# Moving the per-chunk sums over d from place 9 to place 13 in a three-layer cross network kernel

## The chip, the cores and the metric

The kernel runs on one core of a Trainium2 chip. The metric is the device time of one execution in microseconds. Three timed executions of the kernel before gave 656.12, 654.75 and 654.58 us, with a median of 654.75 us. A fourth execution was profiled. Its instructions span 655.7 us and its own time was 657.29 us.

## What is computed

A batch of 512 rows looks up 39 embedding tables and gets x0, of shape (512, 39, 16): batch b, field f, dimension d. Three cross layers follow, each with 128 maps, and the result of each is summed over d. Then comes a small dense network. Cut to what matters:

```python
x0 = xk = e                                   # (512, 39, 16)
for W in (f0, f1, f2):
    z = einsum('bfd,bgd->bfgd', x0, xk).reshape(b, f * g, d)
    cur = einsum('bpd,pm->bmd', z, W)         # (512, 128, 16)
    outs.append(cur); xk = cur
z = sum(concatenate(outs, axis=1), axis=-1)   # over d
h = relu([z, dense_ctx] @ W_top1 + b_top1)
h = relu(h @ W_top2 + b_top2)
y = h @ W_top3
```

Everything is float32. The output is (512, 1).

## The kernel before

**Tiling.** The batch is cut into 16 chunks c of 32 rows (CHUNKS, CB). A chunk has 32 x 16 = 512 columns (b, d). It is cut again into four subs s of 8 rows, which are 128 (b, d) pairs each. Four chunks make a quarter of 128 rows.

**Layer 1** is the main work. For a sub, x1 (128 maps by 128 pairs) is multiplied with w1 for all 39 fields. The 39 x 128 result columns are produced in 10 strips of four fields (the last has three). So a chunk has SLOTS = 40 places n, one strip at each. A strip is three matmuls, high and low parts of the operands (L988, L989, L992). It is written to one of Y_BANKS = 7 PSUM banks, used in turn. Each strip is then multiplied with x0 per field and added into x2. ScalarE (ACT) does strips 0, 3, 5 and 8 of a sub (BY_ACT, L859). VectorE (DVE) does the other six (L718). Its first one, strip 1, starts from the tile that ACT writes from strip 0 (`first`). GpSimd (POOL) adds up the parts (L584 twice, L591, L594) and writes the finished x2 of the sub, transposed, into the tile x2_t (L600; the profile prints x_t for it and for x0_t). POOL also issues the table gathers (L574), until three chunks before the end.

**Layer 0** of the next chunk is woven into the same 40 places. DVE makes six products z at places 9, 12, 15, 18, 21 and 24 (L649), one more at place 6 (L660) and a correction at 27 (L671). TensorE uses them at places 15 to 33 (L948, L935). TensorE also turns x0 at place 6 (L957). Around places 35 to 38, ACT and DVE take the result apart (L803, L691, L696).

**The sums.** Layer 2 is linear in x2, and only its sum over d is wanted. So the kernel first forms g_sum[g, f, b], the sum over d of x2 times x0, and multiplies with w2 afterwards. For chunk c-1 this is `sum_products(c - 1)` (L1006): 32 small matmuls, into four PSUM banks of the same ring of seven (TILES = 4). It stands in front of strip SUMS_AT = 9 of chunk c in TensorE's order. It waits for x2_t of the last sub of chunk c-1 (x2_t_ready), for x0_diag, and, by `drained`, for the four banks that it overwrites. ACT copies the four banks to g_sum in `keep_g` (L826), which stands at the same place in ACT's order. POOL may write x2_t of the first sub of chunk c only when the sums have read the old one (g_ready).

**Layer 2** (L1019, 39 matmuls) is done for a whole quarter at place 13 of chunks 4, 8 and 12 (`closes_quarter`), and for the last quarter after the loop. It needs g_sum of its last chunk.

**Order.** All of this is written out by hand, engine by engine. Every engine executes its list in order and waits on semaphores. There is no planner. The ring positions come from `slot_of_strip` and `slot_of_sums`: strip q sits in slot q + 4 x (sums before it), and its bank is the slot modulo 7. With the sums at place p, the four banks they need were last used by strips p-7 to p-4, and the three strips after the sums reuse those of strips p-3 to p-1.

Of the kernel before, what the change touches and what calls it, by code (L numbers as in the profile page):

```python
# [19 lines left out]
CHUNKS = BATCH // CB  # L20
# [12 lines left out]
PER_QUARTER = CHUNKS // QUARTERS  # L33
# [43 lines left out]
def part_of(c, s):  # L77

    return c + HALVES - 1 if c else s * HALVES // SUBS
# [104 lines left out]
TILE_ROWS = P // TILES  # L184
TILE_B = SB // TILES
TILE_COLUMNS = TILE_B * FG
SUMS_AT = 9
LAST_SUMS_AT = 38
SUMS_OF = [(c, 0, SUBS) for c in range(CHUNKS - 1)] + [(CHUNKS - 1, 0, SUBS - 1), (CHUNKS - 1, SUBS - 1, SUBS)]


def sums_before(q):

    c, n = q // SLOTS, q % SLOTS
    return (c - 1 if c else 0) + (c > 0 and n >= SUMS_AT) + (c == CHUNKS - 1 and n >= LAST_SUMS_AT)


def slot_of_strip(q):

    return q + TILES * sums_before(q)  # L200


def slot_of_sums(e):
    if e == CHUNKS:
        return SLOTS * CHUNKS + TILES * e
    c, at = (e + 1, SUMS_AT) if e < CHUNKS - 1 else (CHUNKS - 1, LAST_SUMS_AT)
    return SLOTS * c + at + TILES * e


STRIP_IN = {slot_of_strip(q): q for q in range(SLOTS * CHUNKS)}  # L210
SUMS_IN = {slot_of_sums(e) + t: (e, t) for e in range(CHUNKS + 1) for t in range(TILES)}


def closes_quarter(c):

    return c > 0 and c % PER_QUARTER == 0


def layer0_at(c):


    plans = []
    if c == 0:
        plans.append((1, PRODUCT0_HALF_AT, LAYER0_HALF_AT, *TURN_X0_HALF_AT, *X1_HALF_AT))
    if c + 1 < CHUNKS:
        product_at, layer_at = PRODUCT0_AT, LAYER0_AT
        if c == 0:
            product_at, layer_at = PRODUCT0_FIRST_AT, LAYER0_FIRST_AT
        elif closes_quarter(c):
            product_at, layer_at = PRODUCT0_LATE_AT, LAYER0_LATE_AT  # L230
        plans.append((part_of(c + 1, 0), product_at, layer_at,
                      *(TURN_X0_AT if c else TURN_X0_LATE_AT), *X1_AT))
    return plans
# [6 lines left out]
def build_program(nc, a):  # L240
    with ExitStack() as ctx:
# [531 lines left out]
        def _(act):  # L773
            def high_last(i):
                k = i - STACKED_FROM
                act.wait_ge(z0_last_ready, k + 1)

                at_least(act, z0_stack_ready, k)
                act.copy(z0_last_hi[:], z0_last[:]).then_inc(z0_last_hi_ready, 1)

            def parts_of_w0_last():
                act.wait_ge(w0_last_ready, 1)
                act.copy(w0_last_hi[:], w0_last[:]).then_inc(w0_last_hi_ready, 1)
                act.wait_ge(w0_last_hi_ready, 1)
                act.wait_ge(roles_in, 16)
                act.activation(w0_last_signed[:], w0_last_hi[:].bitcast(F32), ACT.Copy, scale=roles[:, 1:2]
                               ).then_inc(w0_signed_ready, 1)

            def diagonal(c):
                act.wait_ge(x0_t_ready, part_of(c, SUBS - 1) + 1)  # L790
                act.wait_ge(mask_in, 16)

                at_least(act, g_ready, c)
                for b in range(TILE_B):
                    last = act.activation(x0_diag[:, :, b, 0:FIELDS], x0_t[:, c % 2, :, :], ACT.Copy,
                                          scale=mask[:, b:b + 1])
                last.then_inc(diag_ready, 1)

            def high_x1(i):

                at_least(act, strip_ready, SLOTS * (chunk_of(i) - 1))
                act.wait_ge(l0_step, T0 * i + T0)
                act.copy(x1_hi[:, chunk_of(i) % 2, columns_of(i)], acc0[:, columns_of(i)]).then_inc(x1_hi_ready, 1)  # L803

            def keep_x0_t(i):
                c, subs = chunk_of(i), subs_of(i)

                at_least(act, scale_step, scaled_before(SUBS * (c - 1), 0) if c else 0)
                at_least(act, diag_ready, c - 1)
                act.wait_ge(x0_t_turned, i + 1)  # L810
                act.copy(x0_t[:, c % 2, subs[0]:subs[-1] + 1, :],
                         x0_t_bank[i > 0][:, subs[0]:subs[-1] + 1, 0:FIELDS]).then_inc(x0_t_ready, 1)

            def keep_g(e):

                c, begin, end = SUMS_OF[e]
                act.wait_ge(g_ready, e + 1)
                if begin == 0 and closes_quarter(c):

                    act.wait_ge(out1_ready, c // PER_QUARTER)  # L820
                    act.wait_ge(out2_done, c // PER_QUARTER)
                at = c % PER_QUARTER * CB
                kept = g_sum[:, :, at + SB * begin:at + SB * end].rearrange("g f (s t b) -> g t f s b", t=TILES, b=TILE_B)
                for t in range(TILES):
                    found_sums = strip_flat[:, (slot_of_sums(e) + t) % Y_BANKS, 0:TILE_COLUMNS * (end - begin)]
                    act.copy(kept[:, t, :, :, :], found_sums.rearrange("g (s b f) -> g f s b", b=TILE_B, f=FG)  # L826
                             ).then_inc(g_kept, 1)

            def keep_out1(quarter):
                act.wait_ge(g_kept, kept_of_quarter(quarter))  # L830
                act.copy(out1[:, P * quarter:P * quarter + P], g_sum[:, FIELDS, :]).then_inc(out1_ready, 1)

            def keep_out2(quarter):
                act.wait_ge(out2_done, quarter + 1)
                act.copy(out2[:, P * quarter:P * quarter + P], acc2[quarter]).then_inc(out2_ready, 1)
# [53 lines left out]
            for c in range(CHUNKS):  # L889
                for n in range(SLOTS):  # L890
                    s, g = n // STRIPS, n % STRIPS
                    for i, _, _, _, keep_at, high_at, _, _ in layer0_at(c):
                        if n == high_at:
                            high_x1(i)
                        if n == keep_at:
                            keep_x0_t(i)
                    if (STACKED_FROM <= part_of(c + 1, 0) < X0_PARTS
                            and n == (STACK_LATE_AT if closes_quarter(c) else STACK_AT)[1]):
                        high_last(part_of(c + 1, 0))
                    if (c, n) == W0_STACK_AT:  # L900
                        parts_of_w0_last()
                    if n == DIAGONAL_AT:
                        diagonal(c)
                    if c and n == SUMS_AT:
                        keep_g(c - 1)
                    if c == CHUNKS - 1 and n == LAST_SUMS_AT:
                        keep_g(c)
                    if closes_quarter(c) and n == KEEP_OUT1_AT:
                        keep_out1(c // PER_QUARTER - 1)
                    if closes_quarter(c) and n == KEEP_OUT2_AT:  # L910
                        keep_out2(c // PER_QUARTER - 1)
                    if g in BY_ACT[s]:
                        scale(c, s, g)
# [14 lines left out]
        def _(pe):  # L928
# [22 lines left out]
            def turn_x0(i):  # L951
                c = chunk_of(i)
                pe.wait_ge(once_in[c % 2], 16 * arrivals(i))

                at_least(pe, out0_ready, i)
                for s in subs_of(i):
                    last = pe.transpose(x0_t_bank[i > 0][:, s, :], x0_once[:, c % 2, P * s:P * s + P], ident[:])  # L957
                last.then_inc(x0_t_turned, 1)
# [35 lines left out]
            def sum_products(e):  # L994

                c, begin, end = SUMS_OF[e]
                slot = slot_of_sums(e)
# [45 lines left out]
            for c in range(CHUNKS):  # L1043
                for n in range(SLOTS):
                    s, g = n // STRIPS, n % STRIPS
                    for i, _, layer_at, turn_at, _, _, _, _ in layer0_at(c):
                        if n in layer_at:
                            layer0(i, layer_at.index(n))
                        if n == turn_at:
                            turn_x0(i)  # L1050
                    if c and n == SUMS_AT:
                        sum_products(c - 1)
                    if c == CHUNKS - 1 and n == LAST_SUMS_AT:
                        sum_products(c)
                    if closes_quarter(c) and n == LAYER2_AT:
                        layer2(c // PER_QUARTER - 1)
                    layer1(c, s, g)
# [115 lines left out]
```

## Time and profile before

| what | value |
|---|---|
| median of three executions | 654.75 us (654.58 to 656.12) |
| profiled execution: its own time, its span | 657.29 us, 655.7 us |
| PE busy | 619.1 us, 94% of the span |
| DVE busy | 536.5 us, 82% |
| POOL busy | 515.2 us, 79% |
| ACT busy | 357.9 us, 55% |
| chain that ended last | PE 72%, POOL 18% of the span |
| DMA | 48.86 MB, mean 75 GB/s |

PE is TensorE's matmuls and PEld its weight loads. The profile gives TensorE's granted clock as 0.984 of full speed over the span. In the 40 slices PE shows 9 tenths from the fourth to the last but one. DVE and POOL also show 8 and 9 in most slices. They fall to 5 and 7 tenths in three groups of slices: there TensorE does layer 2 and nothing arrives for them. The chain is the work that ended last, followed back from the end.

### The profile page before, as it was taken

Reading aid. Unit: us, or ns where it says so; the run is one execution under the profiler, and the core shown is the slowest. Engines: PE = TensorE matmul, PEld = TensorE weight load, DVE = VectorE, ACT = ScalarE, POOL = GpSimd, SP = SyncE. Lnnn points to the kernel's source line nnn. Section 1 sums busy time; section 2 is a strip of 40 time slices with the busy share of each in tenths; the row PEclk is TensorE's granted clock in tenths of the full one; section 3 lists DMA queues with packets and bytes.
Section 4 is the critical chain, followed back from the end, with each engine's and each line's share of the span. In section 5 each row is a group of like instructions: output and inputs, shape, how many; then the busy total and the mean of one; then the engine's idle time right before and its main releaser. Section 6 shows DMA issues by size and latency. Waiting matters only on the chain.

```text
span 655.7 us, 11120 instructions
## 1 busy us (share of the span) xinstructions
PE 619.1 (94%) x3096; PEld 468.4 (71%) x3096; DVE 536.5 (82%) x1656; ACT 357.9 (55%) x1200; POOL 515.2 (79%) x486
## 2 busy tenths in 40 slices
PE   0549999999999999999999999999999999999998
PEld 0237677777778777777778777777778777778873
DVE  4129989999995889999995889999995889988911
ACT  4115465656563565756563565756563565756712
POOL 6726888999995999999995999999995997757620
PEclk9859999999999999999999999999999999999999
DMA  7423503823140413224140413223140413100000
GB/s 232 107 56 114 144 14 96 299 50 110 30 129 3 124 35 94 66 44 116 31 127 3 127 31 96 64 48 112 31 128 3 129 30 93 62 1 1 0 1 0
DMA packets 63101, 48.86 MB, mean 75 GB/s; under 512 B 38916, under 2 KB 44428, under 8 KB 62912
## 3 DMA queue, kind: packets, MB, share of 16 engines
q1 hardware_dynamic: 56392, 42.89, 22.7%
q0 software_dynamic: 5120, 1.32, 2.6%
q10 hardware_dynamic: 1528, 3.95, 1.7%
q8 instruction: 24, 0.39, 0.2%
q14 instruction: 37, 0.30, 0.1%
HBM read 46.20 MB, written 1.94 MB: 73 GB/s over the span
## 4 chain that ended last, share of the span: by engine, by line
PE 72%; POOL 18%; another core or an unknown queue 3%; issue 2%; DMA 1%; DVE 1%; ACT 1%; ACTq 1%; SPq 0%; POOLq 0%; DVEq 0%
PE strip L988 17%; PE strip L992 17%; PE strip L989 17%; PE acc L948 10%; POOL found L574 5%; POOL added L584 5%; PE acc L1019 4%; POOL added L591 4%; PE strip L1006 3%; POOL added L594 2%; POOL x_t L600 1%; PE strip L1019 1%; DVE scaled L718 1%; PE strip L1090 1%
## 5 line engine op out<-in xcount | busy, mean ns | idle before, releaser
L718 DVE SCALAR_TENSOR_TENSOR scaled<-strip,x_t,scaled 128x128 f32<-128x128 f32 x1216 | 330.7, 339 | 26.8 <-PE strip L992 26.6
L988 PE MATMUL strip<-w_hi,x_hi 128*128 128x512 f32 (+1 forms) x640 | 291.4, 455 | 3.4 <-ACT x_hi L803 3.4
L992 PE MATMUL strip<-w_hi,x_lo 128*128 128x512 f32 (+1 forms) x640 | 249.7, 390 | 0.0
L989 PE MATMUL strip<-w_lo,x_hi 128*128 128x512 f32 (+1 forms) x640 | 249.5, 390 | 0.0
L584 POOL TENSOR_TENSOR added<-added,product 128x512 f32<-128x512 f32 x128 | 170.0, 1328 | 67.6 <-ACT product L859 62.9
L859 ACT ACTIVATE product<-strip,x_t 128x128 f32<-128x128 f32 x512 | 146.9, 373 | 112.4 <-PE strip L992 109.5
L574 POOL DMA_INDIRECT found<-in_tables,rows x160 | 167.8, 1049 | 28.6 <-issue 13.1
L988 PEld LDWEIGHTS strip<-w_hi,x_hi 128*128 128x128 f32 x640 | 120.8, 189 | 48.5 <-issue 18.0
L989 PEld LDWEIGHTS strip<-w_lo,x_hi 128*128 128x128 f32 x640 | 121.0, 189 | 42.8 <-issue 21.8
L992 PEld LDWEIGHTS strip<-w_hi,x_lo 128*128 128x128 f32 x640 | 120.5, 188 | 26.2
L649 DVE TENSOR_TENSOR z<-shifted,x_thrice 128x512 f32<-128x512 f32 (+2 forms) x105 | 100.8, 963 | 19.7 <-issue 7.7
L948 PE MATMUL acc<-z,w 128*128 128x512 f32 (+2 forms) x210 | 103.3, 575 | 10.4 <-issue 10.4
L859 ACT ACTIVATE added<-strip,x_t 128x128 f32<-128x128 f32 x256 | 73.2, 369 | 69.4 <-PE strip L992 59.7
L718 DVE SCALAR_TENSOR_TENSOR scaled<-strip,x_t,first 128x128 f32<-128x128 f32 x256 | 71.8, 342 | 33.2 <-PE strip L992 26.6
L591 POOL TENSOR_TENSOR added<-added,scaled 128x512 f32<-128x512 f32 x64 | 86.4, 1350 | 5.5 <-DVE scaled L718 2.5
L859 ACT ACTIVATE first<-strip,x_t 128x128 f32<-128x128 f32 x256 | 73.5, 376 | 20.1 <-DVE scaled L718 9.9
L594 POOL TENSOR_TENSOR added<-added 128x256 f32<-128x256 f32 x64 | 53.1, 830 | 5.0
L948 PEld LDWEIGHTS acc<-z,w 128*128 128x128 f32 (+1 forms) x210 | 39.1, 192 | 21.6 <-issue 12.6
L600 POOL TENSOR_TENSOR x_t<-added 128x128 f32<-128x128 f32 x64 | 37.4, 584 | 5.0
L826 ACT COPY g_sum<-strip 128x320 f32<-128x320 f32 (+2 forms) x68 | 24.5, 462 | 11.8 <-PE strip L1006 11.8
L1019 PEld LDWEIGHTS acc<-g_sum,w 128*128 128x128 f32 x234 | 26.6, 192 | 0.3
L1019 PE MATMUL acc<-g_sum,w 128*128 128x128 f32 x234 | 26.6, 275 | 0.0
(67 smaller groups left out, 232.3 us busy)
## 6 DMA issues: line engine op xcount, KB each, us to landing
shifted<-x_fields SPq DMA_DIRECT2D x91, 234.0 KB
x_thrice<-x_fields SPq DMA_DIRECT2D x29, 234.0 KB
shifted_last<-x_fields SPq DMA_DIRECT2D x14, 234.0 KB
found<-in_tables,rows POOLq DMA_INDIRECT x160
w<-in_L_rec_f SPq DMA_DIRECT2D x1, 2496.0 KB
g_sum<-in_L_rec_f ACTq DMA_DIRECT2D x4, 512.0 KB
shifted<-x_fields SPq DMA_DIRECT2D x56, 22.0 KB
shifted<-x_half_fields SPq DMA_DIRECT2D x10, 117.0 KB
```

The source lines that it names most:

```text
L574: pool.indirect_dma_start(out=found[:, c % E_SLOTS, k, :], out_offset=None, in_=a["tables"][:, :], in_offset=bass.IndirectOffsetOnAxis(ap= ...
L584: pool.tensor_tensor(added[:, u % 2, :, :], added[:, u % 2, :, :], product[:, product_slot(u, k) % PRODUCTS, :, :], ALU.add).then_inc(add_ ...
L591: pool.tensor_tensor(added[:, u % 2, :, :], added[:, u % 2, :, :], scaled[:, u % 2, :, :], ALU.add).then_inc(add_step, 1)
L594: pool.tensor_tensor(added[:, u % 2, 0:2, :], added[:, u % 2, 0:2, :], added[:, u % 2, 2:4, :], ALU.add).then_inc(sum_step, 1)
L649: dve.tensor_tensor(z0[of, m % Z_SLOTS, columns], shifted[of, t, columns], (x0_thrice2 if second_side else x0_thrice)[of, p, columns], ALU ...
L718: dve.scalar_tensor_tensor(into, strip[:, slot_of_strip(q) % Y_BANKS, j, :], x0_t[:, c % 2, s, f:f + 1], onto, ALU.mult, ALU.add).then_inc ...
L859: last = act.activation(into[:, j, :], strip[:, slot_of_strip(q) % Y_BANKS, j, :], ACT.Copy, scale=x0_t[:, c % 2, s, f:f + 1])
L948: pe.matmul(acc0[:, columns_of(i)], w0[of, t, :], z0[of, m % Z_SLOTS, columns_of(i)], start=(t == 0), stop=(t == T0 - 1)).then_inc(l0_step, 1)
L988: pe.matmul(into, x1_hi[:, c % 2, columns], hi, start=True, stop=False)
L989: pe.matmul(into, x1_hi[:, c % 2, columns], lo, start=False, stop=False)
L992: pe.matmul(into, x1_lo[:, c % 2, columns], hi, start=False, stop=True).then_inc(strip_ready, 1)
L1019: last = pe.matmul(acc2[quarter], w2[:, f, :], g_sum[:, f, :], start=(f == 0), stop=(f == FIELDS - 1))
```

## The change

`SUMS_AT` becomes 13, but in chunks 4, 8 and 12 the sums stay in front of strip 9. So 12 of the 15 sums that stand inside the chunks move four strips later in TensorE's list: those in chunks 1, 2, 3, 5, 6, 7, 9, 10, 11, 13, 14 and 15. `keep_g` moves with them in ACT's list, from in front of strip 10 to in front of strip 13 (both are ACT's strips). The second sums of chunk 15, at place 38, and those after the loop stay. The functions that number the ring of banks follow. No instruction is added or removed.

```diff
-SUMS_AT = 9
+SUMS_AT = 13
+SUMS_BEFORE_LAYER2_AT = 9
 LAST_SUMS_AT = 38
+def closes_quarter(c):
+    return c > 0 and c % PER_QUARTER == 0
+
+def sums_at(c):
+    return SUMS_BEFORE_LAYER2_AT if closes_quarter(c) else SUMS_AT
 def sums_before(q):
     c, n = q // SLOTS, q % SLOTS
-    return (c - 1 if c else 0) + (c > 0 and n >= SUMS_AT) + (c == CHUNKS - 1 and n >= LAST_SUMS_AT)
+    return (c - 1 if c else 0) + (c > 0 and n >= sums_at(c)) + (c == CHUNKS - 1 and n >= LAST_SUMS_AT)
 def slot_of_sums(e):
-    c, at = (e + 1, SUMS_AT) if e < CHUNKS - 1 else (CHUNKS - 1, LAST_SUMS_AT)
+    c, at = (e + 1, sums_at(e + 1)) if e < CHUNKS - 1 else (CHUNKS - 1, LAST_SUMS_AT)
@@ ScalarE
-                    if c and n == SUMS_AT:
+                    if c and n == sums_at(c):
                         keep_g(c - 1)
@@ TensorE
-                    if c and n == SUMS_AT:
+                    if c and n == sums_at(c):
                         sum_products(c - 1)
```

## Rows read from the trace of the kernel before

**Rows 1.** The page's chain that ended last: shares of the span by engine.
```profile
PE 72%; POOL 18%; another core or an unknown queue 3%; issue 2%; DMA 1%; DVE 1%; ACT 1%; ACTq 1%; SPq 0%; POOLq 0%; DVEq 0%
```

**Rows 2.** Stretches from sums to sums: length; busy PE, PEld, DVE, ACT, POOL; clock; DMA.
```profile
90.19:125.52 35.33, 34.39 (x171) 26.12 (x170) 32.86 (x108) 22.47 (x79) 31.27 (x31) 1.00 0.46 143
125.52:160.63 35.11, 34.60 (x169) 26.03 (x169) 33.55 (x103) 20.92 (x73) 32.63 (x31) 1.00 0.40 115
160.63:195.31 34.68, 34.64 (x169) 26.05 (x169) 33.09 (x103) 20.94 (x72) 32.17 (x31) 1.00 0.30 76
238.33:272.65 34.32, 34.32 (x170) 26.12 (x170) 31.76 (x102) 21.26 (x73) 31.72 (x31) 1.00 0.29 76
567.40:601.29 33.89, 33.89 (x166) 25.72 (x166) 30.94 (x103) 21.06 (x72) 22.24 (x21) 1.00 0.00 1
```

**Rows 3.** The waits: who waited for whom, us in total, times, longest.
```profile
PEld strip L1006 <- POOL x_t L600: 7.5, 10, 1.4
PE strip L1006 <- POOL x_t L600: 3.0, 5, 0.9
```

**Rows 4.** Timeline of PE around the sums of chunks 2, 5, 10: start, us, line.
```profile
125.52 1.13 PE L1006 MATMUL strip<-x_diag,x_t 32*128 32x80 f32 x32 [0.94 <-POOL x_t L600]
...
238.00 0.40 PE L992 MATMUL strip<-w_hi,x_lo 128*128 128x512 f32 x1
238.33 1.13 PE L1006 MATMUL strip<-x_diag,x_t 32*128 32x80 f32 x32
...
419.36 0.40 PE L992 MATMUL strip<-w_hi,x_lo 128*128 128x512 f32 x1
420.27 1.13 PE L1006 MATMUL strip<-x_diag,x_t 32*128 32x80 f32 x32 [0.51 <-POOL x_t L600]
```

**Rows 5.** The chain in order of time: layer 0 on PE, chunks 1 and 2.
```profile
95.54 0.86 PE acc L948 x2
...
136.61 1.06 PE acc L948 x2
```

**Rows 6.** Timeline of POOL at four points of the chunks 4, 5, 8, 10.
```profile
211.40 1.29 POOL L584 TENSOR_TENSOR added<-added,product 128x512 f32<-128x512 f32 x1 [6.74 <-ACT product L859]
...
249.52 1.28 POOL L584 TENSOR_TENSOR added<-added,product 128x512 f32<-128x512 f32 x1 [0.15 <-ACT product L859]
...
341.84 0.46 POOL L600 TENSOR_TENSOR x_t<-added 128x128 f32<-128x128 f32 x1
...
427.80 0.46 POOL L600 TENSOR_TENSOR x_t<-added 128x128 f32<-128x128 f32 x1
```

**Rows 7.** Timeline of DVE and ACT near place 9: chunk 10, then DVE in 13.
```profile
419.00 2.15 DVE L718 SCALAR_TENSOR_TENSOR scaled<-strip,x_t,scaled 128x128 f32<-128x128 f32 x8
421.07 0.92 DVE L649 TENSOR_TENSOR z<-shifted,x_thrice 117x512 f32<-117x512 f32 x1
422.17 0.87 DVE L718 SCALAR_TENSOR_TENSOR scaled<-strip,x_t,scaled 128x128 f32<-128x128 f32 x3 [0.17 <-PE strip L992]
422.94 1.14 ACT L859 ACTIVATE first<-strip,x_t 128x128 f32<-128x128 f32 x4
424.29 1.13 DVE L718 SCALAR_TENSOR_TENSOR scaled<-strip,x_t,first 128x128 f32<-128x128 f32 x4 [1.25 <-PE strip L992]
...
534.36 0.68 DVE L649 TENSOR_TENSOR z<-shifted,x_thrice 117x512 f32<-117x512 f32 x1
535.20 0.87 DVE L718 SCALAR_TENSOR_TENSOR scaled<-strip,x_t,scaled 128x128 f32<-128x128 f32 x3 [0.16 <-PE strip L992]
```

**Rows 8.** Timeline of chunk 1, three engines: the preparation of w0's last part.
```profile
94.98 1.13 DVE L718 SCALAR_TENSOR_TENSOR scaled<-strip,x_t,first 128x128 f32<-128x128 f32 x4 [1.81 <-PE strip L992]
106.58 0.28 DVE L676 TENSOR_TENSOR w_last<-w_last,w_last_mirror 117x128 f32<-117x128 f32 x1
106.89 0.30 ACT L783 CAST w_last_hi<-w_last 117x128 fp32r<-117x128 f32 x1 [3.94 <-DVE w_last L676]
109.77 1.28 POOL L584 TENSOR_TENSOR added<-added,product 128x512 f32<-128x512 f32 x1 [1.48 <-ACT product L859]
```

**Rows 9.** Timeline of DVE and POOL in chunk 10: a product beside an addition.
```profile
429.11 2.14 DVE L649 TENSOR_TENSOR z<-shifted,x_thrice 128x512 f32<-128x512 f32 x1
429.39 1.30 POOL L584 TENSOR_TENSOR added<-added,product 128x512 f32<-128x512 f32 x1
```

More of the change, by code:

```diff
@@ L211 @@
 SUMS_IN = {slot_of_sums(e) + t: (e, t) for e in range(CHUNKS + 1) for t in range(TILES)}
-def closes_quarter(c):
-    return c > 0 and c % PER_QUARTER == 0
 def layer0_at(c):
```

## The prediction

> **What bounds the kernel now.** I read the chain first, then the stretches from sums to sums, the waits, and last the timelines around place 9. The chain is 72% PE and 18% POOL [rows 1]: two engines share the bound. The stretches show where. PE is never idle in chunk 5 to 6 (34.32 us, PE 34.32), while chunks 2 to 3 take 35.11 us with PE 34.60 and POOL 32.63 [rows 2]. POOL's 31 instructions there leave only gaps under 0.2 us between them, which every stretch shows, so POOL is in effect full. PE's missing time is at the sums, where it waits for POOL's x2_t [rows 3].
>
> How long it waits comes from start to start. In chunk 5 the sums start 0.33 us after the last matmul before them (238.00 to 238.33), in chunk 10 0.91 us after (419.36 to 420.27): 0.58 us lost [rows 4]. The same 0.58 stands in chunks 3, 7 and 11. Chunk 2 is the worst, with 0.94 us of idle in its row, 1.01 by starts. In the other seven of the twelve chunks whose sums move, PE doesn't wait. The twelve lose 1.01 + 4 x 0.58 = 3.3 us. The three sums that stay lose 0.1 each. The five waiting chunks also lose 0.2 each at a late z of layer 0 (1.06 against 0.86 for the pair of L948) [rows 5]. All of it is 4.7 us, 0.7% of the span: the most that the change could win.
>
> **What the move brings at the wait.** Strips 9 to 12 now run before the sums, 0.53 + 3 x 0.70 = 2.63 us of PE work. x2_t was at most 1.0 us late, so that wait disappears in all twelve chunks. The matmuls are the same and cost the same.
>
> **Why that is not yet time.** POOL doesn't get faster. In a quarter it stands idle for 6.74 us behind layer 2 (211.40), is still waiting a little for ACT's products in chunk 5 (0.15 us at 249.52), and from there it is full until it writes the last x2_t of chunk 7 (341.84) [rows 6]. This is what the sums of chunk 8 wait for, and these stay at place 9, with layer 2 behind them. POOL's path over this stretch holds nothing that the change shortens. What PE no longer waits for in chunks 6 and 7 it would wait for in chunk 8. So where POOL is full, removing PE's waits is worth about nothing, and new PE waits of the same size cost about nothing. What counts is PE's time where POOL has slack: from layer 2 to place 18 of the next chunk, and the last quarter, where POOL is busy 22 us of 34 [rows 2].
>
> **The new wait.** At place 13 the sums need the banks of strips 6 to 9 (at place 9: those of 2 to 5). Strip 9 is DVE's. Its list there is: scale strips 6 and 7, make z, scale strip 9. In chunk 10, z ends at 421.99, so strip 9 is done by 422.85 at the earliest (0.87 us; the 0.17 of idle before it falls away) [rows 7]. PE would be at the sums at 419.36 + 0.33 + 2.63 = 422.32. It waits 0.6 us. I worked out the same for all twelve chunks: 0.24 in chunks 1, 5, 9 and 13 (in 13: z ends 535.04, strip 9 done 535.90, PE at 535.71, 0.05 us for the signal) [rows 7], 0.35 in 14, none in 15 (no z there), 0.6 in 3, 6, 7, 10 and 11, about 0.65 in 2. Behind the waiting sums stand all further strips. After them strips 13, 14 and 15 reuse the banks of 10, 11 and 12. Strip 11 is drained 0.2 us before strip 14 wants its bank, and strip 12 about when strip 15 does, 3.3 us after the sums start (1.06 + 2 x 0.70 + 0.86 for layer 0). I take 0 for these, with 0.5 us per chunk as the other end.
>
> **ACT and DVE.** The four copies of `keep_g` (1.5 us) stood in front of ACT's strip 10 and held back `first`, so DVE stood idle 1.25 us before strip 11 (1.81 in chunk 1) [rows 7, 8]. At place 13 they start while ACT would wait for strip 13 anyway. They delay strip 13 by some 0.8 us and strip 15 hardly. DVE gains 1.3 to 1.8 us per chunk. That ends the late z's (0.2 us in five chunks). It has one more use, in chunk 1. There ACT stands idle 3.94 us until DVE reaches w0's last part at 106.58, and POOL 1.48 us behind ACT [rows 8]. DVE has no idle between 94.98 and 106.58, so it gets there 1.4 us sooner (strip 21 is the limit), and POOL resumes some 1.3 us sooner.
>
> **POOL's wait on g_ready.** x2_t of the first sub follows the sums. In chunk 10 it starts at 427.80 [rows 6]; the moved sums are done by about 424.1. In chunks 1, 5 and 9 the same slack is about 1.4 us. Nothing, with 0.3 us per chunk as the other end. No DMA is moved, and SP's list doesn't meet the sums.
>
> **The sum,** by quarters:
> - Chunks 1 to 4: PE lost 1.01 + 0.58 + 0.1 at sums, 0.6 at late z's and small turns, 2.3 in all. Now 0.24 + 0.65 + 0.6 = 1.5 of its own. POOL allows it, being 1.3 earlier. Gain 0.8 to 0.9.
> - Chunks 5 to 8: the chain goes through PE until place 18 of chunk 5: +0.25, up to +0.5 if ACT's strip 15 is late for POOL. After that POOL's pace. PE's own losses go from 1.05 to 1.4, also +0.4. Take +0.4.
> - Chunks 9 to 12: the same start, +0.25; PE's own losses fall from 1.7 to 1.4. Take +0.1.
> - Chunks 13 to 15: PE alone counts, 0.24 + 0.35 = +0.6.
>
> Together -0.9 + 0.4 + 0.1 + 0.6 = +0.2 us: span 655.7 to 655.9. On the median of the runs shown, 654.75, that is 655.0 us. The profiled execution's own time (657.29) lies 2.5 us above that median, and I carry over only the difference.
>
> **Rivals.**
> 1. *The bound lifts.* POOL has more slack than its full rows say (its pace partly follows PE), and DVE, freed of 1.3 us, drains strip 9 in time. Then PE loses nothing: 654.75 - 4.4 = 650.3 us. For it: chunk 5 to 6 at 34.32 shows what PE can do. Against: POOL's gaps, and DVE's rows before strip 9, where the freed time hasn't begun. Chance 0.09.
> 2. *The ring jams (slower).* DVE's z at place 12 falls on a POOL addition. A z takes 0.68 us undisturbed [rows 7] and 2.14 beside an addition of 1.30 [rows 9]. Then strip 12 is drained 1.2 us late instead of on time, and strip 15 waits. It decides once DVE needs over 3.3 us from the start of the sums. At the end of 0.5 us for each of 12 chunks: 655.0 + 6 = 661; if it counts only in the four chunks where POOL has slack, 657. Chance 0.14.
> 3. *POOL's pace changes.* DVE's products after place 11 all move by up to 1.4 us against POOL's additions. POOL's stretches of the same 31 instructions differ by 0.45 us (35.11 against 34.68) with z's two places later [rows 2]. Over six full stretches that is 2.7 us either way: 652.3 or 657.7. Chance 0.14, half each side.
>
> The Trainium skill (page "SBUF — State Buffer", the part on who interferes with whom) states that a VectorE operation with two SBUF inputs and a GpSimd operation that reads SBUF lock each other out: the second blocks fully until the first ends. The 2.14 us agree (0.68 + 1.30 and a rest). By that rule an addition caught behind a z could lose up to 0.68 us, and rival 3 would reach twice as far.
>
> **How the numbers follow.** Forecast 0.63 (on its own 653.9 to 656.3), rivals 0.09, 0.14, 0.14. Faster by over 0.3% means under 652.8 us, slower over 656.7; 0.3% is about what a measurement of this kernel tells from no change. Faster: 0.09 + 0.05 of rival 3 + 0.04 of the forecast's tail = 0.18. Slower: 0.10 of rival 2 + 0.04 + 0.02 = 0.16. Same: 0.66. The range 652.2 to 657.6 leaves out rival 1 and the worse end of rival 2.
>
> **What would show it.** Right: no row in which the moved sums wait for POOL, instead a wait for DVE's L718 of 0.2 to 0.6 us; the sums of chunks 4, 8 and 12 waiting for POOL, by up to 1 us in 8 and 12; POOL's 1.48 us in chunk 1 gone; stretches in the last quarter 0.2 to 0.4 us longer. Wrong: no such DVE wait (rival 1), waits at strips 14 or 15 after the sums (rival 2), or POOL's full stretches no longer 35.1 and 34.7 us (rival 3).

## The result

The changed kernel takes 659.58 us (median of nine runs) where the kernel before takes 655.06 (nine runs). The ratio is 1.0056, with a 95% interval of 1.004 to 1.0072. The forecast was 655.0 us, the same within 0.3%, with a range from 652.2 to 657.6. It was wrong: the change makes the kernel slower, by 3.7 us by the ratio.

The profiled executions span 655.7 us before and 658.3 us after. That is 2.6 us and less than the medians say. Up to strip 8 of chunk 1 the profile after is 0.4 us shorter; its mean granted clock is 0.987, that of the profile before 0.984, and in both the clock is lowered only before 50 us. From chunk 1 on, the two can be compared stretch by stretch. Lines of the changed kernel are six higher than before from the helpers on: L994, L995, L998 are a strip, L1012 the sums, L954 layer 0, L724 DVE's strips, L655 its products z, L590, L597 and L600 POOL's additions, and L606 its write of x2_t.

The page after, first the busy times, then the chain by engine and by line:

```profile
PE 618.1 (94%) x3096; PEld 468.3 (71%) x3096; DVE 531.8 (81%) x1656; ACT 355.6 (54%) x1200; POOL 507.2 (77%) x486
...
PE 75%; DVE 15%; another core or an unknown queue 3%; issue 3%; DMA 2%; ACTq 1%; ACT 1%; DVEq 0%
```

POOL's 18% of the chain [rows 1] are gone, and DVE has 15% in its place. PE's waits say where. This is the view of who waited for whom after, us in total, times, longest:

```profile
PE strip L1012 <- DVE scaled L724: 3.6, 11, 0.7
PE strip L994 <- DVE scaled L724: 2.9, 4, 0.7
```

No row of PE names POOL's x2_t any more [rows 3]. The sums wait for DVE in eleven of the twelve moved places. Four strips wait too, and they carry the result. PE's timeline in chunk 13 shows one of them:

```profile
536.45 0.39 PE L998 MATMUL strip<-w_hi,x_lo 128*128 128x512 f32 x1
537.05 1.13 PE L1012 MATMUL strip<-x_diag,x_t 32*128 32x80 f32 x32 [0.21 <-DVE scaled L724]
538.11 0.50 PE L994 MATMUL strip<-w_hi,x_hi 128*128 128x512 f32 x1
...
539.62 1.02 PE L954 MATMUL acc<-z,w 117*128 117x512 f32 x2
541.36 0.51 PE L994 MATMUL strip<-w_hi,x_hi 128*128 128x512 f32 x1 [0.71 <-DVE scaled L724]
```

The sums start 0.60 us after the matmul before them, against 0.33 where nothing waits [rows 4]. Strip 15 (541.36) would be recorded at about 540.1 if nothing held it, right after the start of L954's second matmul, and it waits for the bank of strip 12. This difference is the 1.28 us of the expectations below. It is too large as a loss, because the first matmul of a strip that nothing holds is recorded 0.02 us after L954's second (131.50 and 131.52 in chunk 2); the loss is taken further down from the second matmul. DVE and POOL at that time:

```profile
536.90 1.13 DVE L724 SCALAR_TENSOR_TENSOR scaled<-strip,x_t,first 128x128 f32<-128x128 f32 x4
537.94 2.32 DVE L655 TENSOR_TENSOR z<-shifted,x_thrice 117x512 f32<-117x512 f32 x1
540.19 2.15 DVE L724 SCALAR_TENSOR_TENSOR scaled<-strip,x_t,scaled 128x128 f32<-128x128 f32 x8
...
538.39 1.31 POOL L597 TENSOR_TENSOR added<-added,scaled 128x512 f32<-128x512 f32 x1
```

The product z at place 12 takes 2.32 us, because POOL's addition runs from 538.39 to 539.70. z ends 0.56 us behind it. Strip 12 is scaled only then (540.19 to 541.30), and strip 15 starts at 541.36. The same picture stands in chunks 1, 5 and 9. From the start of L954's second matmul to that of strip 15's second it is 1.64 us there, against 0.66 in an unhindered chunk: 0.98 us lost, four times (in the other chunks whose sums move strip 15 doesn't wait: z at place 12 takes 0.68 us there, 1.32 in chunk 14, and chunk 15 has none).

### The profile page after: what moved, and what is told of

The parts are those of the page before. It is cut to its first block, busy times and chain, and to the rows that moved or that the text cites. A ratio compares the mean times of both kernels' runs of the same rounds, so it can differ in the third digit from the quotient of the medians.

```text
span 658.3 us, 11120 instructions
## 1 busy us (share of the span) xinstructions
PE 618.1 (94%) x3096; PEld 468.3 (71%) x3096; DVE 531.8 (81%) x1656; ACT 355.6 (54%) x1200; POOL 507.2 (77%) x486
## 3 DMA queue, kind: packets, MB, share of 16 engines
q0 software_dynamic: 5120, 1.32, 2.7%
## 4 chain that ended last, share of the span: by engine, by line
PE 75%; DVE 15%; another core or an unknown queue 3%; issue 3%; DMA 2%; ACTq 1%; ACT 1%; DVEq 0%
PE strip L994 18%; PE strip L998 17%; PE strip L995 17%; DVE scaled L724 12%; PE acc L954 11%; PE acc L1025 4%; DVE z L655 2%; PE strip L1012 2%; DMA g_sum<-in_L_rec_f 1%; PE strip L1025 1%; PE strip L1096 1%; PE acc L963 1%; ACTq L883 1%; DVE z_last L666 1%
## 5 line engine op out<-in xcount | busy, mean ns | idle before, releaser
L724 DVE SCALAR_TENSOR_TENSOR scaled<-strip,x_t,scaled 128x128 f32<-128x128 f32 x1216 | 332.8, 344 | 29.9 <-PE strip L998 29.1
L994 PE MATMUL strip<-w_hi,x_hi 128*128 128x512 f32 (+1 forms) x640 | 289.8, 453 | 5.6 <-DVE scaled L724 2.9
L998 PE MATMUL strip<-w_hi,x_lo 128*128 128x512 f32 (+1 forms) x640 | 249.7, 390 | 0.0
L995 PE MATMUL strip<-w_lo,x_hi 128*128 128x512 f32 (+1 forms) x640 | 249.3, 390 | 0.0
L590 POOL TENSOR_TENSOR added<-added,product 128x512 f32<-128x512 f32 x128 | 175.7, 1373 | 80.5 <-ACT product L865 75.9
L580 POOL DMA_INDIRECT found<-in_tables,rows x160 | 163.1, 1020 | 28.4 <-issue 10.3
L994 PEld LDWEIGHTS strip<-w_hi,x_hi 128*128 128x128 f32 x640 | 120.7, 189 | 52.9 <-issue 17.2
L995 PEld LDWEIGHTS strip<-w_lo,x_hi 128*128 128x128 f32 x640 | 121.0, 189 | 41.6 <-issue 20.6
L998 PEld LDWEIGHTS strip<-w_hi,x_lo 128*128 128x128 f32 x640 | 120.6, 188 | 26.1
L954 PE MATMUL acc<-z,w 128*128 128x512 f32 (+2 forms) x210 | 102.4, 571 | 10.6 <-issue 10.5
L655 DVE TENSOR_TENSOR z<-shifted,x_thrice 128x512 f32<-128x512 f32 (+2 forms) x105 | 87.3, 835 | 19.9 <-remote 7.8
L724 DVE SCALAR_TENSOR_TENSOR scaled<-strip,x_t,first 128x128 f32<-128x128 f32 x256 | 72.0, 346 | 37.9 <-ACT first L865 22.6
L597 POOL TENSOR_TENSOR added<-added,scaled 128x512 f32<-128x512 f32 x64 | 83.0, 1296 | 3.3 <-DVE scaled L724 0.8
L600 POOL TENSOR_TENSOR added<-added 128x256 f32<-128x256 f32 x64 | 51.9, 810 | 5.0
L954 PEld LDWEIGHTS acc<-z,w 128*128 128x128 f32 (+1 forms) x210 | 39.4, 191 | 20.0 <-issue 12.6
L606 POOL TENSOR_TENSOR x_t<-added 128x128 f32<-128x128 f32 x64 | 33.1, 517 | 5.0
```

The lines of the kernel that those rows point to most:

```text
L580: pool.indirect_dma_start(out=found[:, c % E_SLOTS, k, :], out_offset=None, in_=a["tables"][:, :], in_offset=bass.IndirectOffsetOnAxis(ap= ...
L590: pool.tensor_tensor(added[:, u % 2, :, :], added[:, u % 2, :, :], product[:, product_slot(u, k) % PRODUCTS, :, :], ALU.add).then_inc(add_ ...
L597: pool.tensor_tensor(added[:, u % 2, :, :], added[:, u % 2, :, :], scaled[:, u % 2, :, :], ALU.add).then_inc(add_step, 1)
L600: pool.tensor_tensor(added[:, u % 2, 0:2, :], added[:, u % 2, 0:2, :], added[:, u % 2, 2:4, :], ALU.add).then_inc(sum_step, 1)
L655: dve.tensor_tensor(z0[of, m % Z_SLOTS, columns], shifted[of, t, columns], (x0_thrice2 if second_side else x0_thrice)[of, p, columns], ALU ...
L724: dve.scalar_tensor_tensor(into, strip[:, slot_of_strip(q) % Y_BANKS, j, :], x0_t[:, c % 2, s, f:f + 1], onto, ALU.mult, ALU.add).then_inc ...
```

## The experiments

Ratios are to the kernel before, in runs on the same chip in turns; the 95% interval stands in brackets. In one set the kernel before took 640.3 us instead of 655 to 657, and the profiles of that set have a mean granted clock of 0.997 to 1.00 instead of 0.984 to 0.987. So only ratios are compared across sets, and stretches of the loop, which ran at full clock on both but for 3.4 us in one profile, named below.

**Which chunks lose.** First the chunk behind layer 2 (and chunk 1) put back, then it alone moved:

```diff
-    return SUMS_BEFORE_LAYER2_AT if closes_quarter(c) else SUMS_AT
+    return SUMS_BEFORE_LAYER2_AT if closes_quarter(c) or c % PER_QUARTER == 1 else SUMS_AT
```

> The sums of chunks 1, 5, 9 and 13 stay at place 9 as well; eight sums move instead of twelve. Theory J (jam): the loss sits in the four chunks behind layer 2 and the first one, where strip 15 waits 1.28 us for the bank of strip 12, because the product z at place 12 takes 2.3 us beside a GpSimd addition. Then this kernel gives back about 4 x 1.3 = 5 us and comes out near the kernel before, 654 to 655.5 us. Theory S (the sums' own wait for the bank of strip 9, in every moved chunk): only a third of the loss goes, about 658 us.

Measured: 656.24 us against 656.60, ratio 0.9991 (0.9978 to 1.0004).

```diff
-    return SUMS_BEFORE_LAYER2_AT if closes_quarter(c) else SUMS_AT
+    return SUMS_AT if c % PER_QUARTER == 1 else SUMS_BEFORE_LAYER2_AT
```

> Only the sums of chunks 1, 5, 9 and 13 move to place 13, the other eleven stay at 9. Theory J: the whole loss is here, 655.1 + 4 to 5 = 659 to 660 us. Theory S: a third of the loss, about 656.5 us. If GpSimd's pace sets the end of each quarter, the 1.28 us of chunks 1, 5 and 9 are all passed on, since they lie before the stretch in which it is full.

Measured: 659.5 us against 656.60, ratio 1.0043 (1.0029 to 1.0057). The four chunks hold most of the loss, as theory J says. The other eight moves bring nothing clear of the noise.

**What makes strip 15 wait.** The product z moved behind strip 12:

```diff
-PRODUCT0_AT = [9, 12, 15, 18, 21, 24]
+PRODUCT0_AT = [9, 13, 15, 18, 21, 24]
```

> The changed kernel with VectorE's second product z moved from before strip 12 to behind it (place 13), nothing else. Theory J: strip 12's bank is free before strip 15 wants it, no row with a 1.3 us wait, time 659.6 - 5 = about 654.5 us. Theory S: the wait for strip 9's bank stays, so the time stays at 659 us or near it.

Measured: 655.54 us against 656.60, ratio 0.9988 (0.998 to 0.9997). PE's waits in it:

```profile
PE strip L1012 <- DVE scaled L724: 3.6, 11, 0.7
```

The wait of the four strips is gone, the eleven waits at the sums are unchanged, and the kernel is 0.7 to 0.8% faster than the changed one. Then the cause of the long z taken away, with VectorE's list as in the changed kernel:

```diff
+                short = u % (SUBS * PER_QUARTER) == SUBS
+                of = (slice(0, 1), slice(0, 64)) if short else (slice(0, PER_STRIP), slice(0, MAPS))
-                pool.tensor_tensor(added[:, u % 2, :, :], added[:, u % 2, :, :], scaled[:, u % 2, :, :],
-                                   ALU.add).then_inc(add_step, 1)
+                pool.tensor_tensor(added[:, u % 2, of[0], of[1]], added[:, u % 2, of[0], of[1]],
+                                   scaled[:, u % 2, of[0], of[1]], ALU.add).then_inc(add_step, 1)
...
```

> The changed kernel, with two of GpSimd's additions cut to 64 columns of 512 and 64 of 256 in the first sub of chunks 1, 5, 9 and 13: part of x2 is not added up there, so those sums are not the reference's. It takes away the operation that the long product z (2.3 us) runs beside, and leaves every list and wait as it is. Theory J with the collision as its cause: that z falls to 0.7 to 1.3 us, strip 15 waits under 0.3 us, time about 655 us (GpSimd's own 2 us saved per quarter are not on the path there). If z stays at 2.3 us, the collision with that addition is not the cause.

Measured: 655.74 us against 656.60, ratio 0.9987 (0.9978 to 0.9996). DVE in chunk 13 (lines three higher here):

```profile
533.38 1.13 DVE L727 SCALAR_TENSOR_TENSOR scaled<-strip,x_t,first 128x128 f32<-128x128 f32 x4
534.42 0.69 DVE L658 TENSOR_TENSOR z<-shifted,x_thrice 117x512 f32<-117x512 f32 x1
535.04 2.39 DVE L727 SCALAR_TENSOR_TENSOR scaled<-strip,x_t,scaled 128x128 f32<-128x128 f32 x8
```

The same z takes 0.69 us in place of 2.32, and no row of PE names strip 15's wait. Both ways of ending the wait give the same time within 0.2 us, one with POOL's work cut and one with all of it, so it is the collision that costs.

**Other places.** The ring says which place is free of waits. Place 12 first:

```diff
-SUMS_AT = 13
+SUMS_AT = 12
```

> The changed kernel with 12 in place of 13 for the same twelve sums. They then overwrite the banks of strips 5 to 8 (8 is ScalarE's, done early), and the three strips behind them reuse those of 9, 10 and 11, all in front of the product at place 12. Theory R (the whole price of place 13 lies in which banks fall to whom): no wait for VectorE at the sums and none at strip 15; against the kernel with the second product behind strip 12 the twelve waits of 0.3 to 0.7 us go too. If nothing else bounds, 0.998 less 3 us / 656: ratio to the kernel before 0.994. Theory G (GpSimd's pace bounds the closing sums once TensorE doesn't wait): the quarters in the middle gain only the 0.6 us by which x2_t is now early at chunks 4, 8 and 12; ratio 0.996.

Measured: 638.93 us against 640.32, ratio 0.9972 (0.996 to 0.9983), less gain than either theory gave. The profile has the jam once, in chunk 1 (DVE and POOL beside PE):

```profile
77.04 2.13 DVE L655 TENSOR_TENSOR z<-shifted,x_thrice 117x512 f32<-117x512 f32 x1
77.32 1.28 POOL L590 TENSOR_TENSOR added<-added,product 128x512 f32<-128x512 f32 x1
80.00 0.80 PE L994 MATMUL strip<-w_hi,x_hi 128*128 128x512 f32 x1 [1.50 <-DVE scaled L724]
```

Here it is the z in front of strip 9 that is held up by an addition. Strip 9 is drained at 79.94, and strip 12, which reuses its bank, waits 1.50 us. From 80.0 on the granted clock was 0.50 for 3.4 us. The wait and the halved clock (3.4 us of work at half speed, 1.7 us lost) are the 3.2 us by which this stretch is longer than in the repeat below (37.45 against 34.30). So "no wait for VectorE" did not hold in this execution. Once more, beside other places, on a third set of runs:

> Place 12 once more, beside places 11, 13 and 14 on one chip. Its first profile had 3.4 us at half the TensorE clock in chunk 1, and its first stretches were longer for it. Theory R: without that, no wait over 0.2 us from chunk 1 on, ratio 0.994 to 0.997; the three middle quarters 145.9 us as in the first profile.

Measured: 651.2 us against 655.77, ratio 0.9934 (0.992 to 0.9947). Why the first set gave less is only partly settled. The profiled execution was its slowest (640.71); four others took 638.7 to 639.2 at a mean clock of 1.00, so the halved clock isn't their reason. Whether they had the jam in chunk 1 no profile shows. In both profiles the middle quarters last 145.9 to 146.0 us. Stretches from sums to sums in the repeat, columns as in [rows 2]:

```profile
125.29:159.59 34.30, 34.30 (x171) 26.12 (x170) 32.00 (x103) 21.38 (x75) 31.88 (x31) 1.00 0.41 115
236.93:271.23 34.30, 34.30 (x170) 26.11 (x169) 33.14 (x103) 21.33 (x74) 31.77 (x30) 1.00 0.31 76
```

PE is busy for the whole of each, and in the repeat no row of its waits names the sums or a strip behind DVE. The long product is still there in chunk 5 (2.29 us from 238.80), but with the sums at place 12 the bank of strip 12 is next used by strip 19, and nothing waits. This version beats both kernels.

```diff
-SUMS_AT = 13
+SUMS_AT = 11
```

> Place 11 for the twelve sums. They overwrite the banks of strips 4 to 7, and strips 11, 12 and 13 reuse those of 8, 9 and 10, all in front of the long product at place 12. Theory R (banks and where the products z stand among them): no wait of over 0.2 us at the sums or the strips behind them, and x2_t is in time (it was at most 1.0 us late, strips 9 and 10 bring 1.2); the same time as place 12, ratio 0.997 or somewhat less. Theory L (later is better for the wait on GpSimd): between the kernel before and place 12.

Measured: 656.23 us against 655.77, ratio 1.0002 (0.9993 to 1.0011). A miss for the rule as I applied it. PE's waits show why:

```profile
PE strip L1012 <- DVE scaled L724: 3.1, 11, 0.4
```

At place 11 the last bank needed is that of strip 7, which DVE drains 2.1 us after PE has finished it. I had looked only at the strips behind the sums. Place 12 needs strip 8 last, which is ACT's and drained 1.2 us after, and DVE's strip 7 with 0.7 us more.

```diff
-SUMS_AT = 13
+SUMS_AT = 14
```

> Place 14. The sums overwrite the banks of strips 7 to 10; strips 14, 15 and 16 reuse those of 11, 12 and 13. Theory R: the wait at the sums goes (strip 9 has 0.7 us more), but strip 15 comes no later than before against VectorE's strip 12, so the 1.3 us of chunks 1, 5, 9 and 13 stay or grow, up to 1.9; the others gain 0.4 each. Ratio to the kernel before 1.003 to 1.006. Theory L: faster than place 13.

Measured: 656.99 us against 655.77, ratio 1.002 (1.0011 to 1.0029), a little under the expected band. The waits moved as expected, none at the sums and a longer one at strip 15 of chunks 1, 5, 9 and 13:

```profile
PE strip L994 <- DVE scaled L724: 4.0, 4, 1.0
```

The changed kernel in the same set:

> The changed kernel itself, on the same chip as the other three of this set. Ratio 1.0056 as measured before.

Measured: 659.91 us against 655.77, ratio 1.0064 (1.0051 to 1.0078). So the order from fast to slow is 12, then 9 and 11, then 14, then 13.

**Both early products later.** In the changed kernel, and in the kernel before:

```diff
-PRODUCT0_AT = [9, 12, 15, 18, 21, 24]
+PRODUCT0_AT = [10, 13, 15, 18, 21, 24]
```

> The changed kernel with VectorE's first two products moved from before strips 9 and 12 to places 10 and 13, behind those strips. Theory R: strips 9 and 12 are drained 0.7 us sooner, the sums' wait for strip 9 falls from 0.6 to 0 to 0.1 us, strip 15 doesn't wait. Ratio to the kernel before 0.994 without, 0.996 with a bound by GpSimd (theory G).

Measured: 642.4 us against 640.32, ratio 1.0033 (1.0021 to 1.0044). The expectation fell. The product now stands before strip 11 and meets a POOL addition. It takes 1.78 us, and strip 14 waits for the bank of strip 11 (chunk 6):

```profile
259.15 1.78 DVE L655 TENSOR_TENSOR z<-shifted,x_thrice 117x512 f32<-117x512 f32 x1
...
261.24 0.40 PE L998 MATMUL strip<-w_hi,x_lo 128*128 128x512 f32 x1
262.02 0.50 PE L994 MATMUL strip<-w_hi,x_hi 128*128 128x512 f32 x1 [0.39 <-DVE scaled L724]
```

> The kernel before (all sums at place 9), with the same two products at places 10 and 13. It tells what these two moves do by themselves. If GpSimd's full stretches are its own work, the waits for x2_t at place 9 stay and the ratio is 0.999 to 1.001. If the products' meeting with GpSimd's additions sets its pace, as chunks of 34.7 in place of 35.1 us in the changed kernel suggest, its waits shrink: 3 us or 0.995.

Measured: 639.22 us against 640.32, ratio 0.998 (0.997 to 0.9989), between the two expectations. PE's wait for x2_t at place 9 falls from 3.0 us [rows 3] to 1.5, with no sums moved and POOL's work unchanged:

```profile
PE strip L1006 <- POOL x_t L600: 1.5, 3, 0.5
```

**Does POOL bound anything?** Place 12 with POOL's third addition cut to a quarter:

```diff
-                pool.tensor_tensor(added[:, u % 2, 0:2, :], added[:, u % 2, 0:2, :], added[:, u % 2, 2:4, :],
+                pool.tensor_tensor(added[:, u % 2, 0:1, 0:64], added[:, u % 2, 0:1, 0:64], added[:, u % 2, 2:3, 0:64],
                                    ALU.add).then_inc(sum_step, 1)
```

> Sums at place 12 as in the first of these, and in every sub GpSimd's third addition cut from 256 columns to 64, which leaves part of x2 out, so the sums are not the reference's. GpSimd has some 2 us less to do per chunk. Theory G: the closing sums no longer wait for it, the three quarters lose 0.5 us or more each against the kernel with place 12 alone, 2 us in all. If GpSimd bounds nothing there any more, the two are within 0.5 us of each other.

Measured: 636.22 us, ratio 0.9943 (0.993 to 0.9957). The two middle stretches answering to those of place 12:

```profile
221.72:256.02 34.30, 34.30 (x170) 26.12 (x170) 32.69 (x103) 21.39 (x74) 30.44 (x31) 1.00 0.30 76
256.02:290.32 34.30, 34.30 (x171) 26.12 (x170) 32.94 (x103) 21.40 (x74) 30.80 (x31) 1.00 0.29 76
```

They are as long as those of place 12 to 0.01 us. From the sums of chunk 4 to those of chunk 8 both profiles of this set take 145.91 us, from there to chunk 12 they take 146.00 with POOL's full work and 145.91 with less. So with place 12 POOL bounds nothing in these quarters, where theory G wanted 0.5 us or more each. But the medians are 2.7 us apart (638.93 and 636.22), and by the expectation they should have been within 0.5. The profiles differ before chunk 4: 1.3 us before strip 8 of chunk 1, and 3.5 us in the first quarter, where only the place 12 profile has the jam and the halved clock. The repeat of place 12, with POOL's full work and no jam, has 103.23 us from strip 8 of chunk 1 to the sums of chunk 4, the lighter kernel 103.28. The ratio of the lighter kernel, 0.9943, is also that of the repeat within the intervals. So the 2.7 us don't come from the middle quarters. What they are in the executions without a profile stays open.

## Why the prediction was wrong

**The wait for x2_t** went in all twelve chunks, as said.

**The new wait at the sums** is there, for strip 9's bank, in eleven chunks and not in 15. Predicted 0.24 in chunks 1, 5, 9 and 13, found 0.27. Predicted 0.35 in chunk 14 and about 0.6 in six others, found 0.37 in 3, 6, 7, 11 and 14, 0.58 in chunk 2 and 0.75 in chunk 10 (start to start, less 0.33). In all 4.3 us against 5.0.

**The step that failed is "I take 0 for these, with 0.5 us per chunk as the other end"**, for the strips behind the sums. They lost 0.98 us in four chunks, 3.9 in all. I had the mechanism as rival 2, with the price of z beside an addition (2.14 us) and the point from which it decides (3.3 us after the sums start). In chunk 13 strip 12 is drained 4.25 us after it (537.05 to 541.30). What I didn't do is look where z would fall. The trace of before gave it, in chunk 13:

```profile
537.33 1.30 POOL L591 TENSOR_TENSOR added<-added,scaled 128x512 f32<-128x512 f32 x1
537.86 1.13 DVE L718 SCALAR_TENSOR_TENSOR scaled<-strip,x_t,first 128x128 f32<-128x128 f32 x4 [1.80 <-PE strip L992]
538.90 1.08 DVE L649 TENSOR_TENSOR z<-shifted,x_thrice 117x512 f32<-117x512 f32 x1
```

DVE stood idle for 1.8 us in front of strip 11, the addition ended at 538.63, and z came behind it. With the idle gone, z falls at about 537.1, just ahead of the addition, and is caught by it. I worked out DVE's times in chunk 10 alone, where POOL's list stands otherwise, and gave the rival 0.14. Its second case, the four chunks at 0.5 us each (657 us), had the right chunks and half the price.

**The cover by POOL failed too.** I held POOL to be full from chunk 5 on and its pace fixed, so that PE's waits would come back at chunks 4, 8 and 12. They didn't. Stretches of the changed kernel:

```profile
128.50:163.18 34.68, 34.37 (x170) 26.15 (x170) 32.26 (x103) 21.05 (x73) 31.71 (x31) 1.00 0.34 88
240.80:276.45 35.65, 34.63 (x170) 26.07 (x170) 33.63 (x103) 21.17 (x73) 31.56 (x31) 1.00 0.28 73
276.45:311.14 34.69, 34.38 (x170) 26.15 (x170) 32.24 (x103) 21.10 (x73) 31.67 (x31) 1.00 0.29 75
572.72:606.58 33.86, 33.86 (x165) 25.71 (x165) 30.24 (x100) 21.04 (x72) 21.59 (x21) 1.00 0.00 1
```

POOL's 31 instructions are busy for 31.7 us where they took 32.6 [rows 2]. In the stretch that starts at chunk 5, the jam at strip 15 and the wait at chunk 6's sums make 35.65 of 34.32. The page after shows z and three of POOL's four tensor operations shorter, with the same work, and one longer (L590):

```profile
L655 DVE TENSOR_TENSOR z<-shifted,x_thrice 128x512 f32<-128x512 f32 (+2 forms) x105 | 87.3, 835 | 19.9 <-remote 7.8
...
L590 POOL TENSOR_TENSOR added<-added,product 128x512 f32<-128x512 f32 x128 | 175.7, 1373 | 80.5 <-ACT product L865 75.9
...
L597 POOL TENSOR_TENSOR added<-added,scaled 128x512 f32<-128x512 f32 x64 | 83.0, 1296 | 3.3 <-DVE scaled L724 0.8
...
L606 POOL TENSOR_TENSOR x_t<-added 128x128 f32<-128x128 f32 x64 | 33.1, 517 | 5.0
```

Before, their means were 963, 1328, 1350 and 584 ns. The move changed where DVE's products and POOL's operations meet. In chunk 10 the z at place 12 shows it, first before, then after:

```profile
425.33 1.79 DVE L649 TENSOR_TENSOR z<-shifted,x_thrice 117x512 f32<-117x512 f32 x1
425.60 0.68 DVE L655 TENSOR_TENSOR z<-shifted,x_thrice 117x512 f32<-117x512 f32 x1
```

Chunks 2, 3, 7 and 11 show the same, and the z at place 15 falls from 2.14 us [rows 9] to 0.9 there. So the move ended collisions in the chunks where POOL is full and made new ones in the four where strip 15 pays for them. That was rival 3, and it came true on the good side. The shorter waits with the products alone moved agree with it. That these meetings are the whole of POOL's 0.9 us per full chunk is argued, not measured apart.

**The account closes** by PE's starts alone. From strip 8 of chunk 1 to the sums of chunk 4 both kernels lost about 2.2 us (105.45 and 105.44 us in all, against 103.23 in the repeat of place 12). From there to the sums of chunk 8: 1.05 against 2.0 (147.04 and 147.97). To chunk 12: 1.7 against 2.4 (147.72 and 148.31). To the second sums of chunk 15: 0 against 1.6 (132.25 and 133.83). Together +3.1 us, where I had -0.9 + 0.4 + 0.1 + 0.6 = +0.2. The kernel with z behind strip 12, which differs in the place of that z and has no jam, took 104.48, 147.00, 147.33 and 132.89 us over the same four parts: -1.0, 0.0, -0.4 and +0.6 against the kernel before, -0.8 together. So the four jams make 3.9 us of difference, 0.98 each, and without them the first and the last term of my sum (-0.9 and +0.6) come out. In the middle quarters the terms of +0.4 and +0.1 were too high, since POOL's pace was not fixed. The first quarter missed its gain because chunk 1 is one of the four with the jam. With z behind strip 12, chunk 1's x2_t arrives 0.7 us sooner (36.04 us from one x2_t to the next, against 36.76 before), so the gain from DVE's freed time exists, but is about half of the 1.3 that I gave it. Some of that time may have come back as waits of DVE for ACT's tile `first`, which grew from 4.7 us to 22.6 over the changed kernel and which I had not counted. The slack at g_ready that I gave as 1.4 us in chunks 1, 5 and 9 is about 2.5 by the starts in the trace before; nothing hangs on it. The medians differ by more than the 3.1 us (4.5, or 3.7 by the ratio). The rest isn't placed; there is one profile of the kernel before on that chip.

## What to carry to other kernels

When a step that takes several buffers of a ring at once is moved, list both the buffers that it overwrites and those that the next steps reuse, and write the drain time of each beside it: here place 13 loses 0.64% and place 12 gains 0.66%, in one set of runs. Before a wait is called covered, work out where each operation behind it will fall against the other engine's, because an idle stretch that goes may have kept two operations apart. An engine without gaps isn't a bound with a fixed pace as long as its operations are longer for meeting another's.

## What the runs showed of the hardware

A DVE product with two SBUF inputs takes 0.68 us alone and 2.32 when a POOL addition of 1.31 us starts 0.45 us after the product's recorded start. It ended 0.56 us behind the addition. In the kernel before, two pairs are recorded with the same distance of 0.28 us, the product first, and end differently. In chunk 13 the product (534.36) takes its 0.68 us and the addition (534.64) takes 1.55. In chunk 10 the product (429.11) takes 2.14 us and the addition (429.39) its 1.30. So the order of the recorded starts does not tell who goes first. The Trainium skill (page "SBUF — State Buffer", section "SBUF: two separate sides") says that whichever starts first gets the shared ports for the whole instruction and the other blocks fully. That one of the two keeps its time and the other waits agrees; which of them was first by the record does not.
